# Weight loads in smaller pieces over three queues, VectorE casts, one add on GpSimd, and another queue rule in the planner of an attention-and-FFN kernel

## The reference

```python
def attn(query, Wq, Wk, Wv, Wo):            # 16 heads of 64
    q, k, v = (einsum('bhsd,hde->bhse', heads(query), W) for W in (Wq, Wk, Wv))
    kv  = einsum('bhsd,bhse->bhde', phi(k), v)
    z   = sum(phi(k), axis=2)
    num = einsum('bhsd,bhde->bhse', phi(q), kv)
    den = einsum('bhsd,bhd->bhs', phi(q), z) + 1e-6
    return merge(num / den) @ Wo

def ffn(x, weight, aux_weight1, aux_weight2, bias):
    return tanh(x @ weight @ aux_weight1 @ aux_weight2 + bias)

x = x + layernorm(attn(layernorm(x)))
x = x + layernorm(ffn(layernorm(x)))
```

## Time and profile before

| what | us |
|---|---|
| median of 2 runs | 1007.67 |
| lowest and highest of them | 1006.64, 1008.70 |
| the profiled execution, whole | 1009.71 |
| its span, first to last instruction, slowest core (core 1) | 1008.2 |
| PE busy in the span | 590.8 (59%) |
| DVE busy | 587.5 (58%) |
| ACT busy | 389.1 (39%) |
| POOL busy | 216.4 (21%) |
| spans of the eight cores | 998.3 to 1008.2 |

### The profile page before, as it was taken

One profiled execution on the slowest core, in us unless ns is written; L12 is line 12 of the kernel. 1 busy time (PEld: TensorE's weight loads), 2 busy tenths in 40 slices (PEclk: granted clock), 3 DMA queues, 4 the chain that ended last, 5 costly groups with the idle time before them and its releaser, 6 DMA issues.

```text
span 1008.2 us, 10951 instructions; the slowest of 8 cores (998.3 to 1008.2 us)
## 1 busy us (share of the span) xinstructions
PE 590.8 (59%) x3392; PEld 303.4 (30%) x3392; DVE 587.5 (58%) x978; ACT 389.1 (39%) x705; POOL 216.4 (21%) x130
## 2 busy tenths in 40 slices
PE   0510567775565875675755655555657658755852
...
GB/s 177 268 212 224 207 65 1 0 1 1 21 63 64 21 67 39 63 43 62 43 63 63 65 166 112 56 1 42 43 63 43 62 63 22 63 45 60 1 42 43
DMA packets 20507, 69.52 MB, mean 69 GB/s; under 512 B 1873, under 2 KB 4049, under 8 KB 20450
## 3 DMA queue, kind: packets, MB, share of 16 engines
...
## 4 chain that ended last, share of the span: by engine, by line
PE 31%; DVE 27%; ACT 16%; issue 12%; DMA 6%; POOL 6%; DVEq 1%; ACTq 0%; SPq 0%; POOLq 0%
PE PS_C L720 11%; PE PS_B L760 7%; DVE ln_bn L472 5%; DVE big_b L736 4%; DVE ln_bn L470 4%; POOL big_b L696 3%; PE PS_C L627 3%; PE PS_C L613 3%; ACT big_b L498 2%; DMA stage<-a 2%; ACT big_b L772 2%; DVE big_b L692 2%; PE PS_A L671 2%; DVE big_b L493 2%; ACT ln_l L481 2%
## 5 line engine op out<-in xcount | busy, mean ns | idle before, releaser
L481 ACT ACTIVATE ln_l<-ln_ag,eps_s 128x1 f32<-128x1 f32 x128 | 37.9, 296 | 354.6 <-DVE ln_ag L474 305.1
L760 PE MATMUL PS_B<-p_b,big_b 128*128 128x512 bf16 x512 | 148.0, 454 | 28.0 <-DVE big_b L749 28.0
L696 POOL TENSOR_TENSOR big_b<-big_b 128x1024 bf16<-128x1024 bf16 x32 | 74.4, 2325 | 406.1 <-DVE big_b L692 371.5
L720 PE MATMUL PS_C<-wo_b,big_b 128*128 128x512 bf16 x512 | 154.1, 469 | 5.1 <-ACT big_b L710 5.1
L781 POOL TENSOR_TENSOR out_b<-big_b 128x1024 f32<-128x1024 f32 x32 | 80.7, 2521 | 298.3 <-DVE big_b L493 287.4
L704 PE MATMUL PS_A<-big_b,kvblk_b 128*128 128x128 bf16 x256 | 32.8, 270 | 106.3 <-POOL big_b L696 89.9
L760 PEld LDWEIGHTS PS_B<-p_b,big_b 128*128 128x128 bf16 x512 | 55.5, 113 | 123.0 <-issue 88.3
L720 PEld LDWEIGHTS PS_C<-wo_b,big_b 128*128 128x128 bf16 x512 | 56.9, 116 | 92.1 <-issue 59.5
L520 PE MATMUL PS_T<-eye_b,xn_tm 128*128 128x128 bf16 x256 | 27.8, 274 | 95.3 <-DVE ln_mb L488 44.2
L736 DVE TENSOR_TENSOR big_b<-x_tm,big_b 128x1024 f32<-128x1024 f32 x32 | 60.9, 1902 | 32.5 <-ACT big_b L498 30.6
L488 DVE TENSOR_SCALAR ln_mb<-ln_ag,ln_r 128x1 f32<-128x1 f32 x128 | 26.4, 207 | 86.3 <-ACT ln_r L484 85.9
...
## 6 DMA issues: line engine op xcount, KB each, us to landing
x_tm<-x SPq DMA_DIRECT2D x64, 512.0 KB, 3.4
y<-out_b POOLq DMA_DIRECT2D x32, 512.0 KB, 3.0
...
stage<-wkvblk SPq DMA_DIRECT2D x2, 512.0 KB, 7.9
stage<-wqblk SPq DMA_DIRECT2D x1, 512.0 KB, 9.0
...
```

Of the source, the lines that this page charges most:

```text
L481: p.op("scalar", lambda e, b2=eb: e.activation(sb["l"][:], sb["ag"][:, 1:2], AF.Ln, bias=b2[:]), reads=[(skey, "ag"), ek], writes=[(skey, ...
L696: p.op("gpsimd", lambda e: e.tensor_tensor(qf2_b[j], qf_b[j], rdenbc_b[j], ALU.mult), reads=[("qf", j), ("rdenbc", j, 0), ("rdenbc", j, 1) ...
L720: p.op("tensor", lambda e, cc=c, h2=hh: e.matmul(PS_C[:, h2 * 512:(h2 + 1) * 512], ctx_b[j][:, cc * 128:(cc + 1) * 128], wo_b[:, cc * 1024 ...
L760: p.op("tensor", lambda e, cc=c, h2=hh: e.matmul(PS_B[:, h2 * 512:(h2 + 1) * 512], xn2f_b[j][:, cc * 128:(cc + 1) * 128], p_b[:, cc * 1024 ...
```

## The change

There are five edits.

1. In the planner, a DMA no longer occupies its engine for 150 ns but a queue of its own (`sync_q`, `scalar_q`, `gpsimd_q`) for its whole planned cost. Two x loads are thus 11.2 us apart in the plan.
2. The 16 MB of large weights come in 32 pieces of 512 KB, dealt out in turn to ACT's, SP's and POOL's queue, each queue with one staging buffer `stq`, and DVE instead of POOL casts them.
3. The small weights share two staging buffers of half the size.
4. The add of x (L736, now L735) goes from DVE to POOL.
5. `out_b` has one buffer instead of two.

```diff
-                em = om["engine"]
+                em = om["engine"] + ("_q" if om["dma"] else "")
                 stm = max(eng_free.get(em, 0.0), dep_ready[m])
                 end[m] = stm + cost[m]
-                eng_free[em] = stm + (150.0 if om["dma"] else cost[m])
+                eng_free[em] = stm + cost[m]
...
-    out_b = [A(f"out_b{i}", [128, D], F32) for i in range(2)]
+    out_b = [A("out_b0", [128, D], F32)]
...
-    stage = [A("stage0", [128, 2048], F32)[:], A("stage1", [128, 2048], F32)[:]]
+    stage = [A("stage0", [128, 1024], F32)[:], A("stage1", [128, 1024], F32)[:]]
+    stq = {q: A(f"stq_{q}", [128, 1024], F32)[:] for q in ("sync", "scalar", "gpsimd")}
...
-    def big_load(queue, src, dst, key, sslot, skey, first_reads):
-        for h in range(4):
-            dma(queue, sslot.rearrange("p (a b) -> p a b", a=2),
-                src.rearrange("(c p) n -> p c n", p=128)[:, 2 * h:2 * h + 2, :],
-                reads=first_reads if h == 0 else (), writes=[skey])
-            p.op("gpsimd",
-                 lambda e, d2=dst, s2=sslot, hh=h: e.tensor_copy(
-                     d2[:, hh * 2048:(hh + 1) * 2048], s2),
-                 reads=[skey], writes=[(key, h)])
...
+    qnames = ("scalar", "sync", "gpsimd")
+    qoff = {"wt": 0, "a1": 2, "a2": 1, "wo": 0}
+    for key, src, dst in (("wt", wt_d, wt_b), ("a1", a1_d, a1_b),
+                          ("a2", a2_d, a2_b), ("wo", wo_d, wo_b)):
+        for h in range(8):
+            q = qnames[(qoff[key] + h) % 3]
+            skey = ("stq", q)
+            dma(q, stq[q].rearrange("p (a b) -> p a b", a=1),
+                src.rearrange("(c p) n -> p c n", p=128)[:, h:h + 1, :],
+                writes=[skey])
+            p.op("vector",
+                 lambda e, d2=dst, s2=stq[q], hh=h: e.tensor_copy(
+                     d2[:, hh * 1024:(hh + 1) * 1024], s2),
+                 reads=[skey], writes=[(key, h // 2)])
...
-        p.op("vector", lambda e: e.tensor_add(x1_b[j], xbuf[:], lnS[j]),
+        p.op("gpsimd", lambda e: e.tensor_add(x1_b[j], xbuf[:], lnS[j]),
...
         p.op("gpsimd", lambda e: e.tensor_tensor(
-            out_b[j][:], x1_b[j], lnS4[j], ALU.subtract),
-             reads=[("x1", j), ("lnS4", j)], writes=[("out", j)])
+            out_b[0][:], x1_b[j], lnS4[j], ALU.subtract),
+             reads=[("x1", j), ("lnS4", j)], writes=[("out",)])
```

53 lines of the change are left out of this document (23 added, 30 removed).

## The result

| | kernel before | kernel after |
|---|---|---|
| median of the runs | 1008.75 us (10 runs) | 1310.0 us (11 runs, 1307.76 to 1314.1) |
| ratio | | 1.298, 95% interval 1.295 to 1.301 |
| profiled execution: its time, its span | 1009.7, 1008.2 us | 1307.6, 1305.9 us |

The account below looks back on a forecast made before the run. The prediction took waits and their order to bound the kernel. Terms 53 + 66 + 44 + 81 = 244 us on 1009.7 gave 1253.7, less 2.0 for the median: 1252 us, with an 8-in-10 range of 1150 to 1300.

Parts of the forecast that it names:

- What bounds it: Whole kernel: no engine busy over 59% of the span, so waits and their order bound it.
- Pass 1, one tile at a time: Pass 1, second sequence: 8 tiles cost their whole chain, 9.8 us in place of 4.31; +44 us.
- Loading and pass 1 of sequence 0: First sequence: DVE starts at about 72 us, last `kf` at 204 instead of 151.70; +53 us, between +41 and +64.
- The bound of 83 us: Loading, first sequence: slow bound for DVE's start, from 200 GB/s and 5.9 us for the x tile.
- fast loads: Loading: rival with three independent queues reaching 462 GB/s, DVE starting near 37 us; 1217 us, chance 0.06.
- Pass 2: Output projection C and FFN product G alternate, period 25.4 us: +66 us in the first pass 2, +81 in the second.
- the locks: Pass 2: rival where POOL operations block DVE's on shared ports, period 26.1 us; 1272 to 1283 us, chance 0.20.
- The single `out_b` costs nothing: Pass 2, output buffer: a store has a period of 25 us to land, so one buffer adds 0 us.
- Chain only: Pass 2: rival where work between C and G fits into its waits, period 21.1 us; 1128 us, chance 0.16.
- DVE relieved: Pass 2 bound by DVE, pass 1 orders free: rival gaining 1.2 us a tile from the add; 967 us, chance 0.03.
- nothing much: Whole kernel: rival where the gain in the load hole pays for the orders, within 2% of before; chance 0.03.

Follow-up runs that it names:

- The runs with fixed lists: Kernel after, all lists kept, one operation exchanged at issue: add of x on DVE, 1287.3 us; last subtraction over 8 of 1024 columns, 1238.4 us.
- the run with the short store: Kernel before with a single `out_b` and a planner that costs a store at 3.0 us in place of 11.2: 1008.1 us, ratio 1.000.
- the run without the subtraction: Kernel after, all lists kept, the last subtraction on POOL run over only 8 of its 1024 columns: 1238.4 us, ratio 1.230.

## Why the forecast had the direction right and the size wrong

**What bounds it.** "The kernel is bound by waits, and the question is in what order they come" was right. Every large part of the loss is an order that the planner chose. Taking back the rule gives 99 us and giving back the second buffer 120, in two runs, and neither changes what an instruction has to do.

**Pass 1, one tile at a time.** Right: 8 serial intervals at 10.03 us (forecast 9.8), +47.6 us (forecast +44).

**Loading and pass 1 of sequence 0.** This is the step that failed most: the term was mis-sized, +80.6 measured for a forecast of +53, above its own upper bound of +64. It is 28 of the 58 us that the forecast was short. Its parts: the first statistics at 88.2 rather than 72; 11.2 rather than 8.5 us from there to the first `kf`, with a table load of 1.28 us on ACT and a cast of `wo` in it; 62.3 rather than 55.2 us for the next eight intervals (the four with a whole chain took 10.6 to 13.0 us, with the statistics of two tiles in most of them, the drained ones 3.4 to 5.2); 70.6 rather than 68.6 us for the last seven. Two errors stand in the 16 us of the start. First, I counted 26 pieces and reckoned 15.3 MB. DVE's list has 28 casts ahead of x, and each queue has one more piece on its way, some 31 pieces: the four stretches sum to 18.0 MB (201, 168, 216 and 225 GB/s over 20, 20, 20 and 28 us). At 229 GB/s these take 79 us. Second, the rate was 205 GB/s and not 229. I took 229 from two streams of 1 MB pieces with POOL casting, but the new loading has one buffer a queue, and the casts take the queues in a fixed order: from 47 us on DVE waits 4.5 to 5.1 us for `stq_gpsimd` in each round of three pieces, and 9.3 us in the last. With a second buffer the rate over the same 88 us was 240. The bound of 83 us that I had from 200 GB/s and 5.9 us was too short for the first reason alone: 18.0 MB at 200 GB/s are 90 us.
The Trainium skill (Trainium Kernel Development and Optimization, Key Constraints) says that the three queues share the same DMA engines. I used it against the "fast loads" rival, and the rival did fail: 205 GB/s over the first 88 us, and 222 before. But it wasn't the shared engines that set the 205 GB/s: they were busy for 0.55 to 0.68 of the four stretches, where before had a share of 0.97 at 306 GB/s, and a second buffer alone raised the rate.

**Pass 2.** C and G alternate, every C directly behind a G, as forecast. The period was 26.0 us for a forecast of 25.4. The term that was mis-sized is the end of C to the start of G: 16.9 us, where I had 14.4 + 1.2 = 15.6. The pair G and C was 9.8 in the forecast and is 26.0 - 16.9 = 9.1. The larger part of what was missing is the locks, which I had put at nothing in the forecast and in a rival: 16.3 us for this distance and 26.1 for the period. That the rival's period is within 0.1 of the measured one is luck, since its distance was 0.6 too short and its pair 0.7 too long. The locks were no second thought but a fixed part of the new order: POOL's operation starts 0.4 to 0.8 us ahead of DVE's in nearly every tile of both passes 2. The runs with fixed lists price them: the add with its lock 0.6 us a tile, the subtraction's lock 1.7 us. The forecast's 1.2 us for the add was too much, because the normalising and a cast stand behind it on DVE in any case. A third thing had no term: C's statistics start 1.4 us after the end of C (983.78 after 982.42), behind those of the tile before, where in the row that gave the 14.4 us it was 0.3. Added up, 14.4 + 0.6 + 1.7 + 1.1 = 17.8 us are 0.9 more than the 16.9, so these parts overlap; no run parts them further.
The Trainium skill (SBUF — State Buffer, Who interferes with whom) says that an operation that takes the port pair shared by VectorE and GpSimd holds it for its whole length and the other blocks. The traces agree: 2.20 and 2.50 us beside POOL, 0.81 without, in the same lists.

**"The single `out_b` costs nothing".** True of the chip, as the run with the short store shows, and wrong as a sentence on the change. The forecast read the alternation from the lists and priced it under pass 2, but named no cause for it. The cause is this buffer, by way of the plan; the rule for the queues leaves pass 2 alone (20.8 and 20.2 us), and the add on POOL by itself makes C C G G.

**The range.** Its upper end, 1300, held the slow period and the +11 of the loading, each taken from one measured neighbour. With the locks in the forecast itself (1272) and the 18.0 MB in the loading (79 us in place of 72, +7) the forecast would have been 1279, and 48 us above it, as wide as the range was, would have held the result. This is reckoned afterwards.

**The other rivals.** "Chain only" fell: the period was 26, not 21. "DVE relieved" and "nothing much" fell with it. With the old rule, two buffers and the add on DVE, the kernel (new loading alone) is still 3 per cent slower than before.

What stays open: the 27 us that the four parts do not add up to, how much of the single buffer's 120 us is locks and how much waits, and the 14 us of the run without the subtraction that lie outside the periods. In the new planner the choice of the next operation still looks at the time of the engine and not at that of the new queue; what that does to the lists was not tried. That a first x load ahead of the weights on SP's queue would save the late start was not tried.
